# One routed block for the rests of three experts, in a mixture-of-experts layer on one core

## The reference

```python
x = x + xattn(ctx_512, layernorm(x), Wq, Wk, gamma)        # (4, 512, 512)
x = x + ffn(layernorm(x), ...)

# ffn: B*S = 2048 tokens, H = 512, I = 352, E = 8 experts, TOP_K = 2
logits = x @ router_w.T
topk_w, topk_idx = top_k(softmax(logits), 2)
topk_w = topk_w / sum(topk_w)
combine[token, topk_idx] += topk_w
for e in experts:
    moe += combine[:, e] * ((silu(x @ gate[e]) * (x @ up[e])) @ down[e])
shared = silu(x @ s_gate + b) * (x @ s_up + b) @ s_down + b
out = moe + shared
```

## Time and profile before

| | us |
|---|---|
| median of 3 runs | 502.76 |
| their lowest and highest | 502.16, 503.51 |
| the profiled execution | 501.43 |
| its span, first to last instruction | 499.7 |
| PE busy in the span | 459.0 |
| DVE busy | 331.0 |
| ACT busy | 260.1 |
| POOL busy | 149.6 |

### The profile page before, as it was taken

How to read it: one execution, slowest core, us unless ns; L and a number is a source line. 1 busy time by engine, 2 the same in 40 slices (tenths; PEclk the granted TensorE clock), 3 DMA queues, 4 the chain that set the end, 5 groups by cost and what they waited for, 6 DMA issues and landing times.

```text
span 499.7 us, 9194 instructions
## 1 busy us (share of the span) xinstructions
PE 459.0 (92%) x2653; PEld 257.7 (52%) x2654; DVE 331.0 (66%) x947; ACT 260.1 (52%) x490; POOL 149.6 (30%) x201
## 2 busy tenths in 40 slices
PE   8528899899999999999989999999999999999980
PEld 3215443454455445554445666666666666666640
DVE  4899989999999999669945665555555433333320
ACT  5899588278627852345444555554545433333330
POOL 3010100031002200410143554555555444444431
PEclk9769999999999999999999999999999999999995
DMA  8832310256023501365388788777777444444441
GB/s 268 273 82 83 131 61 1 84 120 157 0 86 90 80 0 56 119 83 139 104 194 236 184 227 202 179 190 180 187 174 177 84 85 84 84 82 86 84 88 23
DMA packets 39007, 60.55 MB, mean 121 GB/s; under 512 B 8234, under 2 KB 18730, under 8 KB 38963
## 3 DMA queue, kind: packets, MB, share of 16 engines
q0 software_dynamic: 10384, 23.38, 26.3%
q1 hardware_dynamic: 26514, 36.61, 22.8%
q10 hardware_dynamic: 2064, 0.02, 0.2%
HBM read 37.68 MB, written 22.30 MB: 120 GB/s over the span
## 4 chain that ended last, share of the span: by engine, by line
PE 75%; DVE 12%; ACT 4%; DMA 4%; issue 3%; POOL 0%; SPq 0%; DVEq 0%; POOLq 0%
PE bank L1061 6%; PE bank L1063 6%; PE bank L1062 6%; PE bank L1259 4%; PE bank L1256 4%; PE bank L1255 4%; PE bank L1231 4%; PE bank L1232 4%; PE bank L1234 4%; PE bank L1236 4%; PE bank L1235 4%; PE bank L1233 4%; PE bank L1073 3%; PE bank L1200 3%; PE bank L1075 3%; PE bank L1076 3%
## 5 line engine op out<-in xcount | busy, mean ns | idle before, releaser
L568 POOL DMA_INDIRECT out_dram<-xb,sidx x35 | 55.9, 1597 | 81.0 <-ACT xb L909 66.6
L1061 PE MATMUL bank<-xT,W 128*128 128x512 f16 x176 | 66.7, 379 | 0.5 <-DVE sgt L1622 0.5
L1063 PE MATMUL bank<-xT,W 128*128 128x512 f16 x176 | 66.7, 379 | 0.0
L1062 PE MATMUL bank<-xT,W 128*128 128x512 f16 x176 | 66.7, 379 | 0.0
L1757 DVE TENSOR_TENSOR hS<-bank,hS 128x384 f16<-128x384 f32 x35 | 19.4, 556 | 67.9 <-ACT hS L901 67.9
L909 ACT ACTIVATE xb<-bank,wcol 128x512 f32<-128x512 f32 x35 | 24.1, 688 | 54.8 <-PE bank L1259 54.8
L895 ACT ACTIVATE sgt<-bank 128x352 f32<-128x352 f32 x35 | 16.2, 464 | 67.6 <-PE bank L1236 67.4
L1231 PE MATMUL bank<-W,xT 128*128 x136 | 42.5, 313 | 1.2 <-DVE W L1327 1.0
L1236 PE MATMUL bank<-W,xT 128*128 x136 | 42.5, 313 | 0.0
L1235 PE MATMUL bank<-W,xT 128*128 x136 | 42.5, 313 | 0.0
L1232 PE MATMUL bank<-W,xT 128*128 x136 | 42.5, 313 | 0.0
(11 more groups left out here) (271 smaller groups left out, 1031.6 us busy)
## 6 DMA issues: line engine op xcount, KB each, us to landing
out_dram<-W POOLq DMA_DIRECT2D x12, 256.0 KB, 5.0
stage<-L_ffn_down_w_in SPq DMA_DIRECT2D x12, 256.0 KB, 3.5
sim<-L_ffn_down_w_in SPq DMA_DIRECT2D x12, 256.0 KB, 3.6
stage<-L_ffn_gate_w_in SPq DMA_DIRECT2D x16, 176.0 KB, 3.4
stage<-L_ffn_up_w_in SPq DMA_DIRECT2D x16, 176.0 KB, 4.4
sim<-L_ffn_gate_w_in SPq DMA_DIRECT2D x16, 176.0 KB, 3.3
sim<-L_ffn_up_w_in SPq DMA_DIRECT2D x16, 176.0 KB, 4.3
W<-x_in SPq DMA_DIRECT2D x2, 1024.0 KB, 6.7
```

Source lines behind the costliest of these rows:

```text
L568: pool.indirect_dma_start(out=out, out_offset=bass.IndirectOffsetOnAxis(ap=sidx[:, p:p + 1], axis=0), in_=y2[:, p, :], in_offset=None, com ...
L1061: pe.matmul(o, wh, xT[:, 0, c, :], start=(c == 0), stop=False)
L1062: pe.matmul(o, wh, xT[:, 1, c, :], start=False, stop=False)
L1063: last = pe.matmul(o, wl, xT[:, 0, c, :], start=False, stop=(c == KD - 1))
```

## The change

An expert now gets `nblk` = its places / 128, rounded to the nearest number of blocks (the comparison values `k128` begin at 64). Places over that number are `over_`, at most 64. The three experts that come last in a new order (fewest blocks, then most places over) have `cap` = 64, 32 and 32 slots in one shared block, label `MIX_LABEL`, which runs as block `MIXED` = 22; any expert whose `over_` does not fit into its cap gets a further block of its own (`nfull`). `used` is the number of full blocks plus one. The one-hot comparison goes against a row `label`, in which number 22 is the shared block.

For the shared block TensorE runs `mixed_up` and `mixed_down`: each matmul of a normal block becomes three, one per expert, whose outputs lie at partitions 0 to 63, 64 to 95 and 96 to 127 of the same bank. Their weight addresses are constants.

A token can now stand twice in one scatter, once for each of two experts. So `slot_columns` and `merge_slots` form the 128 x 128 matrix of equal tokens, `mixed_parts` copies the block's weighted rows to `ylast`, `mixed_merge` multiplies them by the matrix, inside `routed_up` of block 24, and `mixed_y` copies the sums out for the scatter. `merged_rows`, in VectorE's block 11, sends the second row of a pair to a dummy row (`midx`).

The head has 25 blocks written out, the loop 3 x 2, and two more blocks stand ahead of `rest`, the second with its gate half first. TensorE's waits for weights move to blocks 0, 4, 7, 11, 14, 18, 21 and 22. `BLOCK_AT` has the same units in blocks 0 to 20 as before. The core of the diff:

```diff
 BLOCKS = T * TOPK // P + E - 1
 SURE = 33
-HEAD_BLOCKS = 21
+MIXED = 22
+MIX_LABEL = BLOCKS
+HEAD_BLOCKS = MIXED + 3
+SLOTS = ((E - 1, 0, 64), (E - 2, 64, 96), (E - 3, 96, 128))
+FIRST_USE = [0, 4, 7, 11, 14, 18, 21, MIXED]
...
-BLOCK_AT = [2, 2, 2, 3, 3] + [2] * (HEAD_BLOCKS - 5)
+BLOCK_AT = [2, 2, 2, 3, 3] + [2] * (MIXED - 6) + [0] * 4
...
+    label = below[:, 320:320 + BCOLS]
+    label16 = below[:, 360:360 + BCOLS // 2].bitcast(F16)
+    gap, over_, c5, c6, cap, nfull, where_o, mix_at, nslots, shift = (below[:, 384 + i * E:384 + (i + 1) * E] for i in range(10))
+    merge = below[:, 0:P]
+    merge_later = below[:, P:2 * P]
+    slot_row, later, dummy_off = (below[:, 464 + i:465 + i] for i in range(3))
+    inside = below[:, 0:NT * E].rearrange("p (g e) -> p g e", g=NT)
+    in_mix = below[:, NT * E:2 * NT * E].rearrange("p (g e) -> p g e", g=NT)
...
-            pool.iota(k128, [[P, 16]], base=0, channel_multiplier=0, allow_small_or_imprecise_dtypes=True).then_inc(s_const, 1)
+            pool.iota(k128, [[P, 16]], base=P // 2, channel_multiplier=0, allow_small_or_imprecise_dtypes=True).then_inc(s_const, 1)
...
+            pool.iota(label[:, 0:MIXED], [[1, MIXED]], base=0, channel_multiplier=0, allow_small_or_imprecise_dtypes=True)
+            pool.memset(label[:, MIXED:MIXED + 1], float(MIX_LABEL))
+            link(pool.iota(label[:, MIXED + 1:BCOLS], [[1, BCOLS - MIXED - 1]], base=MIXED, channel_multiplier=0,
+                           allow_small_or_imprecise_dtypes=True))
+            pool.tensor_copy(label16, label).then_inc(s_const, 1)
...
+            if isinstance(j, int) and j == MIXED:
+                pool.wait_ge(s_midx, 1)
+                link2(pool.tensor_copy(sidx[:, p:p + 1], midx[:, :]), s_si, j + 1)
+            else:
+                link2(pool.tensor_copy(sidx[:, p:p + 1], idx[:, bass.ds(j, 1)]), s_si, j + 1)
...
+        def mixed_parts():
+            act.wait_ge(s_y2ps, MIXED + 1)
+            act.wait_ge(d_y[0], 16 * NB)
+            act.activation(ylast[:, 0, :], bank[2 + MIXED % 2][:, :], ACT.Copy, scale=wcol[:, MIXED:MIXED + 1]).then_inc(s_parts, 1)
+        def mixed_y():
+            act.wait_ge(s_merged, 1)
+            act.wait_ge(d_sc[MIXED % 2], 16 * (MIXED // 2))
+            act.activation(y2[:, MIXED % 2, :], bank[2 + MIXED % 2][:, :], ACT.Copy).then_inc(s_y2, 1)
...
+            if isinstance(j, int) and j == MIXED + 2:
+                mixed_y()
...
+            elif isinstance(j, int) and j == MIXED + 1:
+                mixed_parts()
...
+        def mixed_up(j, p):
+            pe.wait_ge(s_x2, j + 1)
+            pe.wait_ge(s_h2, j - 1)
+            for c in range(KD):
+                for s, part in ((0, GU_HI), (0, GU_LO), (1, GU_HI)):
+                    for o, half in ((bank[4 + 2 * p], 0), (bank[5 + 2 * p], I)):
+                        for r, n0, n1 in SLOTS:
+                            w = r * EW + part + c * GU + half
+                            last = pe.matmul(o[n0:n1, 0:I], xT2[:, p, s, c, n0:n1], W[:, w:w + I],
+                                             start=(c == 0 and s == 0 and part == GU_HI), stop=(c == KD - 1 and s == 1))
+            last.then_inc(s_gu2, 1)
+        def mixed_down(j, p):
+            pe.wait_ge(s_h2hi, j + 1)
+            pe.wait_ge(s_y2, j - 1)
+            for s, part in ((0, DN_HI), (0, DN_LO), (1, DN_HI)):
+                if s:
+                    pe.wait_ge(s_h2lo, j + 1)
+                for c in range(DC):
+                    for r, n0, n1 in SLOTS:
+                        w = r * EW + part + c * D
+                        last = pe.matmul(bank[2 + p][n0:n1, :], hT2[:, s, c, p, n0:n1], W[:, w:w + D],
+                                         start=(c == 0 and s == 0 and part == DN_HI), stop=(c == DC - 1 and s == 1))
+            last.then_inc(s_y2ps, 1)
+        def mixed_merge():
+            pe.wait_ge(s_midx, 1)
+            pe.wait_ge(s_parts, 1)
+            pe.matmul(bank[2 + MIXED % 2][:, :], merge, ylast[:, 0, :], start=True, stop=True).then_inc(s_merged, 1)
+        def slot_columns():
+            pe.wait_ge(s_slot_row, 1)
+            pe.transpose(bank[1][:, 0:P], slot_row.to_broadcast([P, P]), ident[:, :]).then_inc(s_slot_cols, 1)
...
+            if isinstance(j, int) and j == MIXED:
+                pe.wait_ge(s_wloD, lows_done(len(UNITS)))
+                mixed_up(j, p)
+                routed_down(j - 1, 1 - p, where(j - 1))
+                return
...
-            elif j % 4 == 0 and j < HEAD_BLOCKS:
-                pe.wait_ge(s_wloD, lows_done(SECOND + j // 4 * PER_EXPERT))
+            elif j in FIRST_USE:
+                pe.wait_ge(s_wloD, lows_done(SECOND + FIRST_USE.index(j) * PER_EXPERT))
...
-            routed_up(j, p, at)
+            routed_up(j, p, at, mixed_merge if isinstance(j, int) and j == MIXED + 2 else None)
...
+            elif not alone and isinstance(j, int) and j - 1 == MIXED:
+                mixed_down(j - 1, 1 - p)
...
+        slot_columns()
         routed_x(0, 0, 0)
...
-            keep_warm(2 if j >= SURE else 4)
+            keep_warm(2)
...
-        link(dve.scalar_tensor_tensor(key, nblk, float(E), io8, ALU.mult, ALU.subtract))
+        dve.scalar_tensor_tensor(key, nblk, 1024.0, io8, ALU.mult, ALU.subtract)
+        link(dve.scalar_tensor_tensor(gap, nblk, float(-P), cnt, ALU.mult, ALU.add))
+        link(dve.tensor_scalar(over_, gap, 0.0, None, ALU.max))
+        link(dve.scalar_tensor_tensor(key, over_, float(-E), key, ALU.mult, ALU.add))
         link(dve.max(sorted_key, key))
         dve.max_index(order.bitcast(U32), sorted_key, key).then_inc(s_order, 1)
-        link(dve.tensor_tensor(above_, key.rearrange("p (o f) -> p o f", o=1).to_broadcast([P, E, E]),
-                               key.rearrange("p (e o) -> p e o", o=1).to_broadcast([P, E, E]), ALU.is_gt))
-        link(dve.tensor_tensor(above_, above_, nblk.rearrange("p (o f) -> p o f", o=1).to_broadcast([P, E, E]), ALU.mult))
+        dve.tensor_scalar(c6, key, sorted_key[:, E - 2:E - 1], None, ALU.is_le)
+        link(dve.tensor_scalar(c5, key, sorted_key[:, E - 3:E - 2], None, ALU.is_le))
+        dve.tensor_tensor(above_, key.rearrange("p (o f) -> p o f", o=1).to_broadcast([P, E, E]),
+                          key.rearrange("p (e o) -> p e o", o=1).to_broadcast([P, E, E]), ALU.is_gt)
+        link(dve.scalar_tensor_tensor(cap, key, sorted_key[:, E - 1:E], c5, ALU.is_le, ALU.add))
+        dve.scalar_tensor_tensor(where_o, c5, 5.0, c6, ALU.mult, ALU.subtract)
+        link(dve.scalar_tensor_tensor(nfull, cap, 32.0, over_, ALU.mult, ALU.is_lt))
+        link(dve.tensor_tensor(nfull, nblk, nfull, ALU.add))
+        dve.scalar_tensor_tensor(where_o, cap, -2.0, where_o, ALU.mult, ALU.add)
+        dve.tensor_scalar(nslots, nfull, float(P), None, ALU.mult)
+        link(dve.tensor_tensor(above_, above_, nfull.rearrange("p (o f) -> p o f", o=1).to_broadcast([P, E, E]), ALU.mult))
+        dve.scalar_tensor_tensor(mix_at, where_o, 32.0, nslots, ALU.mult, ALU.subtract)
         link(dve.tensor_reduce(first, above_, AX.X, ALU.add))
-        dve.tensor_tensor(ends, first, nblk, ALU.add)
-
-        link(dve.scalar_tensor_tensor(slotr, first.rearrange("p (o e) -> p o e", o=1).to_broadcast([P, NT, E]), float(P),
-                                      bank[2][:, 0:NT * E].rearrange("p (g e) -> p g e", g=NT), ALU.mult, ALU.add))
+        dve.tensor_tensor(inside, bank[2][:, 0:NT * E].rearrange("p (g e) -> p g e", g=NT),
+                          nslots.rearrange("p (o e) -> p o e", o=1).to_broadcast([P, NT, E]), ALU.is_lt)
+        dve.scalar_tensor_tensor(in_mix, mix_at.rearrange("p (o e) -> p o e", o=1).to_broadcast([P, NT, E]), float(P * MIX_LABEL),
+                                 bank[2][:, 0:NT * E].rearrange("p (g e) -> p g e", g=NT), ALU.add, ALU.add)
+        link(dve.scalar_tensor_tensor(shift, first, float(P), mix_at, ALU.mult, ALU.subtract))
+        dve.tensor_tensor(ends, first, nfull, ALU.add)
+        link(dve.scalar_tensor_tensor(slotr, shift.rearrange("p (o e) -> p o e", o=1).to_broadcast([P, NT, E]), float(P * MIX_LABEL),
+                                      inside, ALU.subtract, ALU.mult))
+        link(dve.tensor_tensor(slotr, slotr, in_mix, ALU.add))
...
-            link(dve.tensor_tensor(eqh[:, at, :], each(iota16, BCOLS), over(hig16, BCOLS), ALU.is_equal))
+            link(dve.tensor_tensor(eqh[:, at, :], each(label16, BCOLS), over(hig16, BCOLS), ALU.is_equal))
...
-        dve.tensor_copy(used_i[:, :], used_f)
+        dve.tensor_scalar(used_i[:, :], used_f, 1.0, None, ALU.add)
...
+            dve.tensor_tensor(slot_row, rown[:, MIXED:MIXED + 1], zer[:, MIXED:MIXED + 1], ALU.add).then_inc(s_slot_row, 1)
...
+            if isinstance(j, int) and j == MIXED // 2:
+                merged_rows()
...
+        def merge_slots():
+            dve.wait_ge(s_slot_cols, 1)
+            dve.wait_ge(s_slot_row, 1)
```

(38 more changed lines are left out.)

## The result

| | before | after |
|---|---|---|
| median, us (6 runs each) | 502.46 | 509.26 |
| lowest and highest | 502.08, 504.91 | 508.73, 510.95 |
| after / before, 95% interval | | 1.0126 [1.0108, 1.0144] |
| the profiled execution | 501.43 | 510.95 |
| its span | 499.7 | 509.2 |

The changed kernel is slower by 6.8 us, twice the 3.4 of the sum. I first divide the traces, then say what of it holds for the medians.

What follows compares the result with a forecast made beforehand. TensorE's streaming was taken to bound the kernel, 6.28 us per block. -12.6 + 1.9 + 0.4 + 13.7 = +3.4 us on the median of 502.76 gave 506.2 us, range 491.5 to 510.5.

Steps and rivals of the forecast that it cites:

- Two blocks removed, -12.6: Routed blocks: 33 run instead of 35, at 6.28 us of TensorE time each, a gain of 12.6 us.
- third case: Shared block on TensorE: array empties at each of 68 tile-shape changes, plus one stream more per group; +13.7 us, chance 0.50.
- rival 1: Shared block on TensorE: the tiles run side by side, a group takes one stream; 492.5 us, chance 0.31.
- rival 2: Shared block on TensorE: only the two tiles of 32 overlap, and changes are free; 498.0 us, chance 0.05.
- rival 3: Shared block on TensorE: all tiles run in turn without emptying, +11.1 us; 503.6 us, chance 0.07.
- rival 4: Shared block's up and down products: the gaps also lower TensorE's clock, 6 us more; 512 us, chance 0.05.
- rival 5: Routing counts: three more places for one expert make a 34th block run, 6.3 us above whichever case holds; chance 0.02.
- Routing, +1.9: Routing: VectorE's 16 more small operations and later additions delay TensorE by 1.9 us, bounds 0.5 and 3.0.
- Merging product, +0.4: Shared block's merge on TensorE: one f32 matmul of 512 columns, priced from four taking 1.88 us; +0.4 us.
- The conditional jump: In front of the last close: TensorE still has a queue of matmuls and the others wait for it; nothing taken.
- The scatter chain at the end as before: End of the kernel: the tail has the same form, so the chain of last scatters only moves forward.
- The late scatter of the shared block and the weights: Blocks 21 to 27: a scatter some 2 us later and sooner waits for expert weights cost nothing.

Runs made afterwards that it cites:

- experiment 2: Against the changed kernel: all 64-wide matmuls first, then the pairs of 32, 6 changes of width instead of 68; 502.39 us, 0.9997 of before.
- experiment 10: Against the changed kernel: the three further pairs of blocks behind the condition replaced by one more close, so the jump is short; 504.14 us in one run.
- the fall-through: Against the changed kernel: condition turned round, so the last close follows directly and TensorE's jump stands behind it; 505.79 us, 1.0060 of before.
- experiment 12: Against the changed kernel, with its three tiles: the close of block 32 put in front of the condition; 506.14 us, 1.0069 of before.
- experiment 3: Against the changed kernel: the shared block's three tiles become one of 128 output rows, two experts' products left out; 495.07 us, 0.9843 of before.
- experiment 4: Against the changed kernel: two tiles of 64 output rows instead of 64, 32 and 32, third expert's products left out; 494.5 us in one run.

## Why the prediction was right or wrong

The forecast of slower held, and 509.26 us lies in the range. The size was half of what came, by one step. That it lies in the range is in part luck: the room up to 510.5 was left for dearer tiles and a dearer routing, and what filled it was the jump, for which nothing was left.

**Two blocks removed, -12.6.** Right: 33 scatters instead of 35, and an ordinary block takes what it took.

**Shared block, +13.7 by the third case.** Right in its mechanism, 0.75 too large: 12.95 us. One more stream per group and about 0.11 us per change of shape, where the sum had 0.12. The row with the one change in the trace of before gave the price, 0.07 to 0.13. That it came out so near is partly luck: the change there is in a tile's rows and not its columns, and at a granted clock of 7 tenths. The starts of the 64-wide matmuls are 0.53 us apart (0.54 was given) and the up product takes 12.56 (13). The Trainium skill's rule ("TensorEngine Tiling (Array Packing)", section "Key Properties"), by which changing the tiling mode drains the engine and changing the tile doesn't, agrees with the runs on both sides: 0.11 us per change of width, and hardly anything between tiles of one width (3.69 us for 96 matmuls of 32 against 3.58 for 24 of 128).

**The rivals on the tiles.** Side by side (rival 1) holds for tiles of one width only; with four of 32 the change gives 496.9 us with its jump and 492.4 without, and 492.5 was rival 1's time. That only the two of 32 overlap (rival 2) is true as to the overlap, but changes aren't free; experiment 2 is that rival's case with few changes. The Trainium skill's factor for three tiles ("TensorE: Matmul & The Clock Gate", section "Measured speedup vs the span model") had led to an estimate of 1.26 streams per group; in a long row of groups of four the runs show 3.69 / 3.58 = 1.03; three of one width were not run. In turn (rival 3): no. That the gaps lower the clock (rival 4): not in the products, where the granted clock is 1.00; the clock does fall to its lower level of 1.2 GHz, but at the jump's gap of 4.88 us. A 34th block (rival 5): no.

**Routing, +1.9.** Right within what runs tell. VectorE's added operations take 2.65 us in the trace (222.61 to 226.97 against 221.65 to 223.36; 2.5 was the estimate), and TensorE's wait for the one-hots grew from 0.6 to 1.8:

```profile
PE bank L1167 <- DVE W L1805: 1.8, 1, 1.8
```

Block 18 stands at 381.4 us on the average of the twelve traces of kernels with the new routing (380.6 to 382.8), and at 379.7 in the two without: +1.7.

**Merging product, +0.4.** Too small: 0.86 us. The earlier trace rows counts four records, and a matmul of 512 f32 columns leaves two records, 0.43 us each, so those 1.88 us were two matmuls and not four. The program has 16 such instructions at that line where the trace of before counts 32 records, which could have been seen before.

**The conditional jump, "I take nothing for it".** This is the step that failed. Its reason was that TensorE still has a queue of matmuls there. The jump started at 484.4 and TensorE's last queued matmul at 485.27, so the queue covers 1 us of 4.76; the next matmul starts at 490.46. Then the clock is down, and most of the close runs at half speed. From its first matmul to its end the close takes 5.6 us, against 4.0 with the short jump of experiment 10. The traces say +5.8 us. The medians say less: the change minus the same with the close first is 509.26 - 506.14 = 3.1, minus the fall-through 3.5, minus the kernel without the condition 3.7, and on the kernel before the jump alone gives 6.4. By the difference of each to its own kernel before, they are 3.7, 3.1 and 4.0. Ahead of the close, the jump over the same three pairs varies from 3.6 to 4.8 us between the traces, and the trace of after has the longest (behind the close up to 5.2). So 3 to 4 us is what it costs in a common execution of the change, as far as these medians tell; why the kernel before loses 6.4 at the same place is open beyond its second stall.

The terms as measured: -12.6 + 1.7 + 12.95 + 0.86 and 0.4 in the blocks beside them are +3.3, with 3.5 for the jump +6.8, the difference of the medians. The 3.5 is itself taken from the medians, so this sum can't confirm it. With the jump out of the way the total holds: it said +3.4 us, and experiment 12 measured 1.0069, +3.5 us (+3.1 by the medians). That it holds so well is partly luck: routing and tiles were 0.95 too high, the merging product and the blocks beside it 0.86 too low. And in its trace the tail is 1.35 us longer than before, which the medians don't show on top of the 3.3.

**The scatter chain at the end as before.** Wrong in after, since its last link waits for the late close, and by 1.3 us in experiment 12 too. The late scatter of the shared block and the weights stopped TensorE nowhere, as predicted: in 400 to 480 us it has no wait for another engine.

## What to carry to other kernels

Put matmuls of column tiles of one width together: tiles of one width share a stream (four of 32 cost within 0.11 us in 3.6 what one of 128 costs), and each change of width costs 0.11 us and the overlap. Before code is moved to the other side of a jump, look at the jump's own row on each engine's sequencer, also where it costs nothing now; on TensorE it belongs behind the last matmul that anyone waits for. Count instructions in the program before a row's time is divided by its count.

## What the runs showed of the hardware

- TensorE's taken jump took 0.23 us over one close and 2.23 over a pair of blocks (one trace each), 3.57 to 5.16 over two or three pairs without an order between them, and 0.08 to 0.09 when it wasn't taken. VectorE, ScalarE and GpSimd took 0.03 to 0.06 us for the jumps on the same condition in their own programs. Whether distance or the fetching of code decides wasn't separated.
- Behind a gap of 4.88 us in TensorE's work the granted clock was at the lower of its two levels (1.2 and not 2.4 GHz): 512-column f16 matmuls started 0.43 us apart instead of 0.22, until the last ones. Behind the gap of 3.04 us in experiment 3 it was down too, for the first part of the close, and behind the 2.70 of experiment 4 it was not.
- Column tiles of one width overlap almost fully: 24 matmuls of 128 output rows, 48 of 64 and 96 of 32 took 3.58, 3.70 and 3.69 us. A change between widths 64 and 32 costs 0.11 us at full clock, and the tiles on its two sides don't overlap.
- A scatter of 128 rows lands after 4.5 to 5.2 us near the end of every trace, but in seven of the fourteen traces one of the last five scatters took 5.7 to 6.4.
